# Decoder layer, cross-attention stage: similarity and c2q taken as fp32 matmuls on the contexts as loaded, c2q alone transposed

## What is computed

```
cq = jnp.einsum('bcd,bqd,d->bcq', c, q, w_cq) + b_cq
s = (c @ w_c + b_c)[:, :, None] + (q @ w_q + b_q)[:, None, :] + cq
a = jax.nn.softmax(s, axis=2)
c2q_att = jnp.einsum('bcq,bqd->bcd', a, q)
b_att = jax.nn.softmax(jnp.max(s, axis=2), axis=1)
q2c_att = jnp.einsum('bc,bcd->bd', b_att, c)[:, None, :]
x = jnp.concatenate([c, c2q_att, c * c2q_att, c * q2c_att], axis=-1)
z = x @ W_l.T + b_l
```

## Time and profile before

| | us |
|---|---|
| median of 3 runs | 750.28 |
| lowest and highest | 747.78, 754.99 |
| the profiled execution | 753.16 |
| its span on the core | 751.3 |
| PE busy in it | 697.4 |
| attention rounds 2 to 6, each | 50.2 |

### The profile page before, as it was taken

The page is one execution under the profiler, slowest core; times in us unless marked ns, Lnnn a source line. Parts: engine busy times, 40 slices in busy tenths (PEclk is TensorE's granted clock), DMA queues, the critical chain, the costliest instruction groups (busy, mean ns, idle before and its releaser), DMA issues. The chain is left out here.

```text
span 751.3 us, 13182 instructions
## 1 busy us (share of the span) xinstructions
PE 697.4 (93%) x4424; PEld 615.0 (82%) x4424; DVE 522.2 (70%) x1240; ACT 408.5 (54%) x923; POOL 351.8 (47%) x482
## 2 busy tenths in 40 slices
PE   3879999999999999999999966999999999999997
PEld 2768889888989898889898854888888888888886
DVE  5686786877876878778768755767566667666442
ACT  4865775867786768577767433434343343333331
POOL 2656755856758568567585212222223323232222
PEclk9987999999999999999999997899999999999999
DMA  7632321322312313223001057022222203121200
GB/s 214 177 95 67 110 81 53 96 64 83 105 49 84 104 29 118 65 73 115 24 22 53 2 166 251 1 113 85 113 85 96 98 18 126 56 113 57 114 29 29
DMA packets 50768, 64.47 MB, mean 86 GB/s; under 512 B 3800, under 2 KB 49416, under 8 KB 49840
## 3 DMA queue, kind: packets, MB, share of 16 engines
q1 hardware_dynamic: 50736, 64.06, 26.8%
HBM read 56.60 MB, written 7.45 MB: 85 GB/s over the span
## 5 line engine op out<-in xcount | busy, mean ns | idle before, releaser
L1440 POOL TENSOR_TENSOR sg<-sg,cw_wide 128x512 f32<-128x512 f32 x56 | 73.7, 1316 | 186.7 <-ACT sg L1397 177.0
L1401 ACT ACTIVATE a_hi<-af 128x512 fp32r<-128x512 f32 x63 | 39.8, 632 | 154.7 <-DVE af L1521 154.7
L76 PE MATMUL bank<-h_hi,w_lo 128*128 128x512 f32 x224 | 92.5, 413 | 6.3 <-DVE w_lo L1538 4.8
L77 PE MATMUL bank<-h_lo,w_hi 128*128 128x512 f32 x224 | 90.1, 402 | 0.0
L78 PE MATMUL bank<-h_hi,w_hi 128*128 128x512 f32 x224 | 89.8, 401 | 0.0
L1521 DVE TENSOR_TENSOR af<-bank,sg 128x512 f32<-128x512 f32 x63 | 43.2, 686 | 62.0 <-POOL sg L1440 57.6
L820 POOL TENSOR_TENSOR ctxt_lo<-ctxtf,ctxt_hi 128x375 fp32r<-128x375 f32 x64 | 57.7, 924 | 59.3 <-ACT ctx_hi L607 50.8
L825 POOL TENSOR_TENSOR ctx_lo<-ctxf,ctx_hi 125x256 fp32r<-125x256 f32 x96 | 74.5, 804 | 0.0
L1526 DVE TENSOR_TENSOR a_lo<-af,a_hi 128x512 fp32r<-128x512 f32 x63 | 48.1, 763 | 34.9 <-ACT a_hi L1401 34.9
L76 PE MATMUL bank<-w_hi,a_lo 128*128 128x256 f32 x224 | 63.2, 282 | 0.0
L77 PE MATMUL bank<-w_lo,a_hi 128*128 128x256 f32 x224 | 63.2, 282 | 0.0
(11 more groups left out here) (250 smaller groups left out, 2297.1 us busy)
## 6 DMA issues: line engine op xcount, KB each, us to landing
cw_wide<-cw_scratch SPq DMA_DIRECT2D x7, 2048.0 KB, 6.9
ctxtf<-in_ctx_t SPq DMA_DIRECT2D x32, 375.0 KB
ctxf<-in_ctx SPq DMA_DIRECT2D x32, 375.0 KB
xt<-in_x SPq DMA_DIRECT2D x8, 448.0 KB, 3.6
x_scratch<-x2b SPq DMA_DIRECT2D x8, 448.0 KB, 3.2
x2n<-x_scratch SPq DMA_DIRECT2D x7, 512.0 KB, 4.6
x2t<-x_scratch SPq DMA_DIRECT2D x7, 512.0 KB, 3.9
out_dram<-x2t SPq DMA_DIRECT2D x7, 512.0 KB, 3.0
```

The lines of the kernel that those rows point to most:

```text
L76: pe.matmul(dst, a_lo, b_hi, start=first, stop=False, **kw)
L77: pe.matmul(dst, a_hi, b_lo, start=False, stop=False, **kw)
L1401: act.activation(a_hi[n % (AHEAD + 1)][:, :], af[(p + n) % 2][:, :], ACT.Copy).then_inc(a_hi_ok, 1)
L1440: pool.tensor_tensor(sg[b][:, :], sg[b][:, :], cw_wide[p][:, ORDER[n], :], ALU.mult).then_inc(sgw_ok, 1)
```

## The change

Similarity and c2q are taken as fp32 matmuls, directly on `ctxtf` and `ctxf` as they land. All high and low parts of the contexts, of `ctw` and of the softmax numerators go; ACT now copies the transposed numerators into a plain tile `at`. c2q alone is transposed (two transposes a stream for four); c*c2q is formed on the transposed side by DVE, from PSUM and `ct`, and its high and low parts are made apart from those of c2q. `z_c2q` is split in `z_c2q` and `z_x3`. The context of the next round is loaded into a stream's tiles once c2q of that stream is done.

```diff
+            x4_hi, x4_lo = sb("x4_hi", [P, G, KB, L], F32R), sb("x4_lo", [P, G, KB, L], F32R)
...
+            at = sb("at", [SB, G, NSB * L])
...
-                            sp.wait_ge(cx_lo_ok, G * i + j + 1)
+                            sp.wait_ge(c2q_mm, G * i + j + 1)
...
                     def similarity(j):
-                        pe.wait_ge(cw_lo_ok, ev[j])
+                        pe.wait_ge(cx_in[j], 32 * (i + 1))
+                        pe.wait_ge(ctw_ok, ev[j])
                         pe.wait_ge(c_lo_ok, ev[j])
-                        pe.wait_ge(cxt_lo_ok, ev[j])
                         for k in range(KB):
-                            last = mm3(pe, bank[j][0:L, 0:SP_], cw_hi[:, j, k, :], cw_lo[:, j, k, :], ctxt_hi[:, j, k, :],
-                                       ctxt_lo[:, j, k, :], k == 0, k == KB - 1)
+                            last = pe.matmul(bank[j][0:L, 0:S], ctw[:, j, k, :], ctxtf[:, j, k, :], start=(k == 0), stop=(k == KB - 1))
...
                     def c2q_product(j):
-                        pe.wait_ge(cx_lo_ok, ev[j])
-                        pe.wait_ge(a_lo_ok, ev[j])
+                        pe.wait_ge(at_ok, ev[j])
                         for b in range(NSB):
...
+                            last = pe.matmul(bank[j][0:L, 0:D], at[:, j, b * L:(b + 1) * L], ctxf[0:SB, j, b, :], start=(b == 0),
+                                             stop=(b == NSB - 1))
...
                     def turn_x(j):
-                        pe.wait_ge(x3_ok, ev[j])
-                        for k in range(2 * KB):
+                        pe.wait_ge(c2q_ok, ev[j])
+                        for k in range(KB):
...
+                    def z_x3(j):
+                        pe.wait_ge(x3_lo_ok, ev[j])
+                        for k in range(KB, 2 * KB):
...
-                def context_hi(i, j):
-                    act.wait_ge(cx_in[j], 32 * (i + 1))
-
-                    act.activation(ctxt_hi[:, j, :, 0:S], ctxtf[:, j, :, :], ACT.Copy)
-                    act.activation(ctx_hi[:, j, :, :], ctxf[0:SB, j, :, :], ACT.Copy).then_inc(cx_hi_ok, 1)
...
-                        act.wait_ge(ctw_ok, ev[j])
-                        act.activation(cw_hi[:, j, :, :], ctw[:, j, :, :], ACT.Copy).then_inc(cw_hi_ok, 1)
...
                     if not last:
                         residual(i + 1)
...
+                    c2q_copy(0)
+                    c2q_copy(1)
+                    x_high(0)
+                    c2q_copy(2)
...
-                def context_t_lo(i, j):
-                    pool.wait_ge(cx_hi_ok, G * i + j + 1)
-                    for k in range(KB):
-                        last_lo = pool.tensor_tensor(ctxt_lo[:, j, k, 0:S], ctxtf[:, j, k, :], f32(ctxt_hi[:, j, k, 0:S]), ALU.subtract)
-                    last_lo.then_inc(cxt_lo_ok, 1)
...
-                    def cw_low(j):
-                        pool.wait_ge(ctw_ok, ev[j])
-                        pool.wait_ge(cw_hi_ok, ev[j])
-                        pool.tensor_tensor(cw_lo[:, j, :, :], ctw[:, j, :, :], f32(cw_hi[:, j, :, :]), ALU.subtract).then_inc(cw_lo_ok, 1)
...
-                    def a_low(j):
-                        dve.wait_ge(a_hi_ok, ev[j])
...
+                    def x3_product(j):
+                        dve.wait_ge(x_hi_ok, ev[j])
+                        dve.tensor_tensor(tmp[j][:, D:D + KB * L].rearrange("p (k t) -> p k t", k=KB),
+                                          bank[j][:, 0:KB * L].rearrange("p (k t) -> p k t", k=KB), ct[:, j, :, :], ALU.mult).then_inc(x3_ok, 1)
```

More of the change, by code:

```diff
@@ L558, in group @@
                     c2q_product(2)
+                    turn_x(0)
                     c2q_product(3)
+                    turn_x(1)
                     if not last_group:
                         turn_h_pair(i + 1, 0)
-                    turn_x(0)
-                    turn_x(1)
+                    z_c2q(0)
+                    turn_x(2)
                     pe.wait_ge(mrow_ok, i + 1)
-                    turn_x(2)
+                    turn_x(3)
                     for j in range(G):
@@ L569, in group @@
                     last.then_inc(b_mm, 1)
-                    turn_x(3)
-                    z_c2q(0)
                     z_c2q(1)
+                    z_x3(0)
+                    z_c2q(2)
+                    z_x3(1)
                     if not last_group:
@@ L575, in group @@
                         turn_h_pair(i + 1, 1)
-                    z_c2q(2)
                     z_c2q(3)
+                    z_x3(2)
+                    z_x3(3)
                     if last_group:
@@ L673, in exp_similarity, with c2q_copy, x_high, x3_high @@
                                        accum_out=ssum2[:, j:j + 1]).then_inc(exp2_ok, 1)
-                    def a_high(j):
+                    def c2q_copy(j):
+                        act.wait_ge(c2q_mm, ev[j])
+                        act.wait_ge(sinv2_ok, ev[j])
+                        act.activation(tmp[j][0:L, 0:D], bank[j][0:L, 0:D], ACT.Copy, scale=sinv2[:, j:j + 1]).then_inc(c2q_ok, 1)
+                    def x_high(j):
+                        act.wait_ge(t_x, ev[j])
+                        act.activation(op_hi[j][:, 0:KB * L], bank[j][:, 0:KB * L], ACT.Copy).then_inc(x_hi_ok, 1)
+                    def x3_high(j):
+                        act.wait_ge(x3_ok, ev[j])
+                        act.activation(op_hi[j][:, KB * L:2 * KB * L], tmp[j][:, D:D + KB * L], ACT.Copy).then_inc(x3_hi_ok, 1)
+                    def a_columns(j):
                         act.wait_ge(t_a, ev[j])
-                        act.activation(op_hi[j][0:SB, 0:NSB * L], bank[j][0:SB, 0:NSB * L], ACT.Copy).then_inc(a_hi_ok, 1)
+                        act.activation(at[:, j, :], bank[j][0:SB, 0:NSB * L], ACT.Copy).then_inc(at_ok, 1)
                     def wl_high(part):
@@ L737, in group @@
                     exp_similarity(1)
-                    a_high(0)
+                    a_columns(0)
                     exp_similarity(2)
-                    a_high(1)
+                    a_columns(1)
                     exp_similarity(3)
-                    a_high(2)
-                    a_high(3)
+                    a_columns(2)
+                    a_columns(3)
                     if not last:
                         residual(i + 1)
[L746 to L752, removed]
+                    c2q_copy(0)
+                    c2q_copy(1)
+                    x_high(0)
+                    c2q_copy(2)
+                    act.wait_ge(mneg_ok, i + 1)
+                    act.activation(mexp[:, :], m_bank[0:G, 0:L], ACT.Exp, bias=mneg[:, :], accum_out=msum[:, :]).then_inc(mexp_ok, 1)
+                    x_high(1)
+                    c2q_copy(3)
                     if not last:
                         h_high_pair(i + 1, 0)
[L755 to L762, removed]
+                    x3_high(0)
+                    x_high(2)
+                    x3_high(1)
+                    x_high(3)
+                    if last:
+                        act.wait_ge(shared_in, 48)
+                        act.activation(shared_hi[:, 0:GU + D], shared_f[:, :], ACT.Copy).then_inc(shared_hi_ok, 1)
+                    x3_high(2)
+                    x3_high(3)
                     if last:
@@ L1121, in group @@
                         normalise_h(i + 1)
-                    for j in range(G):
-                        dve.wait_ge(c2q_ok, ev[j])
-                        dve.tensor_tensor(tmp[j][0:L, D:2 * D], tmp[j][0:L, 0:D], c[:, j, :], ALU.mult).then_inc(x3_ok, 1)
-                        if j == 0 and last:
-                            moments3(dve, 0)
-                        if j == 2:
-                            dve.wait_ge(mexp_ok, i + 1)
-                            dve.reciprocal(minv[:, :], msum[:, :]).then_inc(minv_ok, 1)
-                            dve.wait_ge(minv_ok, i + 1)
-                            dve.tensor_scalar(mrow[:, :], mexp[:, :], minv[:, 0:1], None, ALU.mult).then_inc(mrow_ok, 1)
+                    x_low(0)
+                    x3_product(0)
+                    if last:
+                        moments3(dve, 0)
+                    dve.wait_ge(mexp_ok, i + 1)
+                    dve.reciprocal(minv[:, :], msum[:, :]).then_inc(minv_ok, 1)
+                    x_low(1)
+                    dve.wait_ge(minv_ok, i + 1)
+                    dve.tensor_scalar(mrow[:, :], mexp[:, :], minv[:, 0:1], None, ALU.mult).then_inc(mrow_ok, 1)
+                    x3_product(1)
                     if not last:
                         h_low_pair(i + 1, 0)
-                    for j in range(G):
-                        dve.wait_ge(x_hi_ok, ev[j])
-                        dve.tensor_tensor(op_lo[j][:, 0:2 * KB * L], bank[j][:, 0:2 * KB * L], f32(op_hi[j][:, 0:2 * KB * L]),
-                                          ALU.subtract).then_inc(x_lo_ok, 1)
+                    x3_low(0)
+                    x_low(2)
+                    x3_product(2)
+                    x3_low(1)
+                    x_low(3)
```

(4 more changed lines are left out.)

95 lines of the change are left out of this document (24 added, 71 removed).

## The result

| | before | after |
|---|---|---|
| median, us | 751.22 | 760.13 |
| lowest and highest, us | 747.78, 754.99 | 759.8, 763.41 |
| span of the profiled execution, us | 751.3 | 761.6 |
| PE busy in it, us | 697.4 | 696.1 |

The account below looks back on a forecast made before the run. PE, busy 93% of the span, was taken to bound the kernel. Round 0 -8, waits in the middle -5.6 and late xt +11.3 summed to -2.3 us: median from 750.3 to 748.0, range 737 to 760.

Parts of the forecast that it names:

- PE's own work: Every round on PE: fp32 similarity and c2q +0.25 us each a stream, fewer transposes -0.75 a round, net +1.25 a round.
- The rival with records at their upper bound: PE's fp32 matmul records cost 0.85 us a stream, +11 on the sum, 759 us; chance 0.05.
- Waits that go: Similarity no longer waits for cw_hi and cw_lo; end of stream 0's c2q 0.8 us sooner a round, -5.6 in seven.
- The walk of the prediction: PE's steps in round 3 from 206.04: similarity(2) from 210.1, stream 0's c2q ending at 216.0, not 216.83.
- The end of a round: After stream 0's c2q: matmuls and transposes cancel, PE waits 1.5 us for the c2q copy; costed at 0 (0 to +0.5).
- Round 0: First round: context copies, POOL's context work and waits go, some half clock returns; -8 us (bounds -3 and -12).
- Late xt: xt, queued behind four context loads and the store, lands at T0 + 21.7; DVE waits 3.9; +11.3 us (0 to +20).
- DVE's reserve: Between DVE's first xt statistics and first score maximum, 5.7 us, 1.7 was waiting and absorbs that much lateness.
- round 7 loads no next xt: Last round: x4's low part follows the store, at T0 + 25.4, ahead of PE's want at about T0 + 27.
- nearly cancel: Likeliest case, whole kernel: the gains and the late xt nearly cancel, range 742 to 755 us; chance 0.50.
- The late xt costs more: Past T0 + 23 PE pays every further microsecond in six rounds; about 760 us, slower than before; chance 0.20.
- The extra that the prediction counted by columns: PE's fp32 for fp32r exchange by columns alone: 0.63 us a stream, 20 in all, 4 above the term used.

Follow-up runs that it names:

- Run 7: The kernel before with only the similarity taken in fp32, c2q and its transposes as before; 749.78 us, ratio 0.998.
- run 4: The kernel before with the 125-partition load of ctxf made in two, of 120 and 5 partitions; 750.4 us, ratio 1.0012.
- run 8: The kernel before with each context load also waiting for its stream's c2q, and the store of x2 ahead of the loads; 763.03 us, ratio 1.0138.
- run 1: The changed kernel with the 125-partition load of ctxf made in two, of 120 and 5 partitions; 743.58 us, ratio 0.990.
- the copy's edit: The changed kernel with c2q_copy of streams 0 and 1 ahead of ACT's residual: 762.22 us; with ctxf also loaded in 120 and 5 partitions: 738.11 us.
- run 9: The changed kernel with SP's order changed to store of x2, contexts 0 and 1, xt, then contexts 2 and 3; 743.96 us, ratio 0.9902.
- Run 2: The changed kernel with the store of x2 moved ahead of the four context loads in SP's order; 756.32 us, ratio 1.0067.

## Why the prediction went wrong, point by point

**PE's own work: right.** The fp32 pairs and what follows them, in round 5 of the kernel after:

```profile
317.90 1.43 PE L474 MATMUL bank<-ctxtf,ctw 128*112 128x375 f32 x4
319.17 0.48 PE L481 MATMUL bank<-ident,tmp 112*125 112x112 f32 x3
320.19 1.46 PE L487 MATMUL bank<-ctxf,at 125*112 125x256 f32 x6
321.49 0.48 PE L481 MATMUL bank<-ident,tmp 112*125 112x112 f32 x3
```

1.27 us for a similarity and 1.30 for a c2q, +0.24 and +0.25 a stream where 0.25 and 0.25 were taken. The rival with records at their upper bound (0.85 a stream) falls.

**Waits that go: right in kind, smaller.** T0 came 0.46 sooner in a steady round and not 0.8; 3.9 in all, inside the bounds (2 to 9). Run 7 shows the parts: 0.70 for the similarity, of which the first fp32 c2q takes 0.25 back. The walk of the prediction holds up to similarity(2), which began 0.35 later than it had it: at 315.56, that is 4.41 us behind turn_c(1) (311.15), where the prediction had 210.1 - 206.04 = 4.06.

**The end of a round: right.** T0 to s is 16.14 for 15.82, +0.3 with bounds of 0 and 0.5 (the sum of +0.4 has 1.6 in it that the kernel before lost at half clock in round 1); the wait of PE for the copy is 1.5 us in each round, as said.

**Round 0: right, its excess not shown to be the change's.** -10.4 for -8 (bounds -3 and -12). The trace of before that it is measured against was slow in round 0: 61.05 at a mean granted clock of 0.89. The same matmuls in run 4 took 57.02 at 0.97 and in run 8 58.26 at 0.94, so the gain to 51.30 is 5.7 to 9.8, by the execution that one takes.

**Late xt: this term failed.** The sum had +11.3 (bounds 0 and +20), the trace has +22.8 in the same stretch. Its parts, 22.7 together: (a) xt lands at T0 + 23.3 and not 21.7. In round 5 the first context took 7.1 us from its issue and not 6.0, while the next one's transposed form ran beside it, and the next three landed 4.4, 4.4 and 4.8 apart where 4.2 was taken. The store and xt together were 0.7 quicker than their term. DVE's reserve was 0.6 better than taken (it absorbs 2.3): the prediction added up busy times that overlap, 4.0 us from the first statistics to the first maximum, and without waits this takes 3.38 (344.88 to 348.26). PE's T0 to s was 0.3 longer. A steady round pays 2.9 and not 2.1 (by the prediction's own numbers, 3.9 less 1.7, it would be 2.2), round 1 2.0 and not 0.8, and round 2, where xt is issued at T0 + 15.9 and lands at s + 8.5, 4.2: 17.8 over six rounds. (b) Stretches at half clock that start behind the new waits and last past DVE's delay: 2.1, in rounds 2 and 4. A window of round 5 shows the level:

```profile
295.00:298.00 3.00, 2.70 (x10) 2.58 (x11) 2.67 (x7) 2.12 (x9) 3.00 (x5) 0.50 0.00 0
```

In round 5 it cost nothing: that round and round 6, which has no such stretch, both take 53.00, since DVE's delay sets their length. (c) Round 7: 2.8. The prediction had x4's low part at T0 + 25.4, ahead of PE's T0 + 27; it came at T0 + 27 in steady rounds, hidden by xt, and at s + 12.4 in round 7, which waits for no xt and so had no cover. The step "round 7 loads no next xt" was true and missed what else the store holds up.

**Put at nothing in the sum: behind the last T0.** The feed-forward part's first x2 was loaded behind the late loads too, and DVE's statistics of it stand ahead of `mrow`: a wait of 2.6, and T0 to the end is 1.4 longer.

**The rivals.** The likeliest case (nearly cancel) did not happen. "The late xt costs more" did, at the time that it gave (about 760), but by another mix: xt was 1.6 us later and not 2.3, round 7 and the clock did the rest, while in the traces round 0 gave more and not less. Its own terms (+25, -5.6 and -12 on 750.3) give 758 and not 760. So the mechanism that it names was at work, and that its number was met is in part luck.

**The rule on fp32 and the rule on engines.** The Trainium skill (FP8 and Floating Point Precision, TensorE Precision Notes) has true fp32 as four passes; the trace agrees, with 1.27 us for 4 x 2 x 375 columns, 1.25 by columns alone. The extra that the prediction counted by columns, 0.63 us a stream, did not come: the rows give 0.24 + 0.25 = 0.49, since the three fp32r matmuls that were replaced took longer than their columns (1.03 and 1.05 us for 0.94 and 0.96). The Trainium skill (DMA: Bandwidth & Descriptors, Why a DMA increments its semaphore by 16 and not by 1) has the outer dimension's largest divisor up to 16 as the number of engines; run 1 agrees, with a share of 1.07 for 0.34.

## What to carry to other kernels

When a change moves the point at which a buffer comes free, list everything behind the affected loads in the same queue and place each arrival against the moment it is wanted, in the first, a middle and the last round: the round without the largest wait is where the second largest shows. Put in the queue first what is wanted first, and look at the partition count of a load before trusting its bytes. Do not judge an edit while a later fixed arrival sets the round: the copy's edit gained nothing before that was cured and 5.5 us after.

## What the runs showed of the hardware that was not expected

- An issue on SP took 0.39 us into an idle queue, and single ones took 3 to 4 with two or more contexts under way (3.00 at 332.82 in the kernel after, 4.09 at 264.08 in run 9), so that all behind them was issued later too. Run 2 shows that this comes with the transfers' own time and not on top: with the store's issue (3.00) out of the way xt came 0.5 to 1.2 us sooner in rounds 2 to 6.
- Five transfer engines alone moved 22 to 24 GB/s each, sixteen together 16.5 (264 GB/s): using three times the engines shortened the whole sequence of loads from 23 us to 17.
- Stretches at the 1.2 GHz level come and go between rounds with the same waits (round 6 of the kernel after had none, round 5 one of more than 3 us, that of the window at 295.00). What sets them off was not settled.
